# A first attention whose score tiles are no longer computed twice on TensorE

## The reference

```python
# first attention: 16 heads of 16 columns
q, k, v = split((x @ w_in.T + b_in).reshape(b, l, 16, -1), 3, axis=-1)
att = softmax(einsum('blhd,bmhd->blmh', q, k) * 0.25, axis=2)
opt = einsum('blmh,blhd->blhd', att, v)          # m is summed over att alone
x = layernorm(x + opt @ w_out.T + b_out)
# second attention: 4 of 16 heads of 64 columns, chosen for each batch
idx = sort(top_k(softmax(mean(x @ Wr + br, axis=1)), 4))
Qs, Ks, Vs = the chosen heads of x @ Wq + bq, x @ Wk + bk, x @ Wv + bv
O = softmax(Qs @ Ks.T / 8) @ Vs
x = layernorm(x + O @ Wo + bo)
```

## Time and profile before

| | |
|---|---|
| median of 3 runs | 3679.16 us (3677.96 to 3679.68) |
| the profiled execution's own time | 3678.28 us |
| its span, first to last instruction | 3676.2 us |
| TensorE (PE) busy | 3442.9 us (94%) |
| VectorE (DVE) busy | 3328.6 us (91%) |
| ScalarE (ACT) busy | 2863.5 us (78%) |
| mean granted clock of TensorE | 0.983 of full speed |

### The profile page before, as it was taken

The page is one execution under the profiler, slowest core; times in us unless marked ns, Lnnn a source line. Parts: engine busy times, 40 slices in busy tenths (PEclk is TensorE's granted clock), DMA queues, the critical chain, the costliest instruction groups (busy, mean ns, idle before and its releaser), DMA issues. The chain is left out here.

```text
span 3676.2 us, 45342 instructions
## 1 busy us (share of the span) xinstructions
PE 3442.9 (94%) x14524; PEld 1301.0 (35%) x14524; DVE 3328.6 (91%) x5273; ACT 2863.5 (78%) x3137; POOL 1872.8 (51%) x1299
## 2 busy tenths in 40 slices
PE   8999998899999999899999999899999999899998
PEld 3444443332232234343332324343332324343333
DVE  7999999999999998889999998879999998567776
ACT  5999999878888887778888887778888887333333
POOL 4344343414454547455454547445454546658775
PEclk9999999899999999899999999999999999999999
DMA  5222221300000002101010001101000100100000
GB/s 168 92 86 90 86 86 61 87 21 18 18 29 15 23 18 63 54 18 29 18 29 14 26 18 58 59 18 29 18 26 13 29 18 26 43 1 12 12 12 12
DMA packets 117214, 142.83 MB, mean 39 GB/s; under 512 B 33394, under 2 KB 100466, under 8 KB 116978
## 3 DMA queue, kind: packets, MB, share of 16 engines
q1 hardware_dynamic: 116978, 139.95, 12.4%
HBM read 89.55 MB, written 50.33 MB: 38 GB/s over the span
## 5 line engine op out<-in xcount | busy, mean ns | idle before, releaser
L1163 ACT ACTIVATE scores<-scores,nmax 128x2048 f32<-128x2048 f32 x1024 | 2042.4, 1996 | 297.4 <-DVE scores L1391 286.1
L1018 PE MATMUL ps<-stack 96*128 96x512 bf16 x4852 | 1314.0, 388 | 116.2 <-DVE scores L1391 86.2
L1391 DVE TENSOR_SCALAR_CACHE_REDUCE scores<-ps,lows 128x1024 f32<-128x1024 f32 x1024 | 1274.8, 1277 | 45.1 <-PE ps L1018 42.5
L920 POOL TENSOR_TENSOR facc<-facc,probs 128x1024 f32<-128x1024 f32 x443 | 1048.0, 2366 | 487.0 <-ACT probs L1302 416.6
L1391 DVE TENSOR_SCALAR_CACHE_REDUCE scores<-ps 128x1024 f32<-128x1024 f32 x1024 | 1214.6, 1217 | 52.2 <-PE ps L1018 46.9
L1018 PEld LDWEIGHTS ps<-stack 96*128 96x128 bf16 x4852 | 374.5, 99 | 1174.6 <-DVE scores L1391 687.8
L1448 DVE TENSOR_REDUCE smax<-ps 128x2 f32<-128x1024 f32 x512 | 620.3, 1219 | 131.4 <-PE ps L1083 129.9
L1083 PE MATMUL ps<-fk,fq 64*128 64x512 f32 x2048 | 562.5, 631 | 48.5 <-DVE smax L1448 30.9
L1098 PE MATMUL ps<-fq,fk 64*128 64x512 f32 x2048 | 550.2, 615 | 10.0 <-DVE smax L1448 4.1
L1118 PE MATMUL ps<-probs,vals 128*64 128x512 f32 x2048 | 527.4, 612 | 0.2
L1302 ACT ACTIVATE probs<-ps 128x1024 f32<-128x1024 f32 x384 | 383.2, 1012 | 66.9 <-PE ps L1101 66.4
(11 more groups left out here) (136 smaller groups left out, 2335.5 us busy)
## 6 DMA issues: line engine op xcount, KB each, us to landing
stack<-qk_levels SPq DMA_DIRECT2D x768, 64.0 KB, 2.2
qk_levels<-fk SPq DMA_DIRECT2D x64, 384.0 KB, 2.4
probs<-in_L_attn_x SPq DMA_DIRECT2D x16, 512.0 KB, 3.9
v_rows<-vals SPq DMA_DIRECT2D x16, 512.0 KB, 2.6
vrows<-v_rows SPq DMA_DIRECT2D x16, 512.0 KB, 3.4
res<-in_L_attn_x SPq DMA_DIRECT2D x16, 512.0 KB, 3.9
x_rows<-y SPq DMA_DIRECT2D x16, 512.0 KB, 2.9
res<-x_rows SPq DMA_DIRECT2D x16, 512.0 KB, 3.9
```

The costliest lines, as they stand in the source:

```text
L920: pool.tensor_tensor(total, total, probs[:, slot, :], ALU.add).then_inc(facc_ready, 1)
L1018: last = pe.matmul(bank(banks[i]), stack[0:SK, hd % 2, 0, t * P:(t + 1) * P], stack[0:SK, hd % 2, 1, col:col + CH], start=True, stop=True)
L1163: act.activation(row, row, ACT.Exp, bias=nmax[:, k % LOWS:k % LOWS + 1], scale=-1.0, accum_out=esum[:, b % 2, t, hd:hd + 1]).then_inc(exp_ ...
L1391: dve.tensor_scalar(scores[:, k % ROW_SLOTS, half * TILE:(half + 1) * TILE].rearrange("p (a n) -> p a n", a=2), two_banks(banks), 1.0, fir ...
```

## The change

The rule, the set and the second matmuls go. `plan()` no longer adds 0.43 us to any tile, so its simulated TensorE is free earlier, and the orders that it writes differ from the first doubled tile on. The line numbers of what follows fall by up to 5 (L1018 becomes L1013, L991 L986, L985 L980, L976 L971, L1055 L1050).

```diff
-NEAR = 12
...
-    again = set()
...
-                twice = n[1] == "A" and queued and not any(m[1] in mode for m in order["PE"][-NEAR:])
-                if twice:
-                    again.add(n)
-                switch = 0.43 * twice + 0.1 * (mode.get(n[1], 0) != now_mode)
+                switch = 0.1 * (mode.get(n[1], 0) != now_mode)
...
-    return order, held, freed, again, now
+    return order, held, freed, now
...
-        order, held, freed, again, planned = plan()
+        order, held, freed, planned = plan()
...
-                    for i in (0, 1, 0, 1) if n in again else (0, 1):
+                    for i in (0, 1):
```

## The result

The changed kernel takes 3702.6 us in the median of 4 runs (3700.39 to 3705.82), the kernel before 3678.86 (3677.96 to 3679.68): a ratio of 1.0065, 95% interval [1.0053, 1.0077]. It is slower by 24 us; the forecast was 18 us more than before, at 3697.

A forecast was written before the change was run, and what follows sets the result against it. The prediction took VectorE's reading of tiles to bound batch 0's first attention. Chunks +12 and seams +6 made +18 us on 3678.3, about 3697 beside the median; its own range was 3685 to 3723 us (0.63).

The forecast's parts named there:

- The bound: Batch 0's first attention: it ends when VectorE has read its tiles, one per 1.175 us; freed TensorE time is worth nothing.
- The clock falls in plain runs, and that alone is free: Batch 0's first attention: clock at 0.50 in longer plain runs; a tile then takes 0.94 us, under VectorE's 1.175.
- The price of a chunk: Batch 0's first attention, twelve chunks: low-clock projections cost 1.5 us in 9, +12 net; ends -1.4 and +36.
- the event: Profile before, near 305 us: one q projection at low clock made VectorE wait 1.08 and 0.36 us, 1.44 together.
- I put this at nothing: Batch 0's first attention: packed projections come closer together on ScalarE, 95% busy; expected cost nothing.
- either way: Batch 0's first attention: VectorE starts a tile every 1.175 us with or without the second matmuls.
- The seams, +6: Seams of batches 0, 1 and 2: FK projections start at low clock, +2 us each; ends -5.4 and +9.
- A: Rival, chance 0.23: nothing late, as the clock stays up or ready tiles cover low projections; about 3677 us.
- B: Rival, chance 0.10: faster, since doubled tiles were in the way of the seams; about 3667 us.
- C: Rival, chance 0.04: TensorE becomes the bound at low clock throughout batch 0's first attention; +122 us, 3800.

The follow-up runs named there:

- warm-start kernel: Changed kernel with second matmuls only for the last six tiles before a chunk's transposes and those between transposes and q projection (137 tiles): 3693.06 us, 1.0046.

## Why the prediction was right, and where it was not

- **The bound.** Right. Batch 0's first attention ends when VectorE has read its tiles, and the TensorE time that was freed (146 us by the prediction's estimate at full clock) bought nothing there.
- **The clock falls in plain runs, and that alone is free.** Right, and shown: 68.1 us at 0.50 with VectorE busy throughout, and in the warm-start kernel low clock almost without waits.
- **The price of a chunk: 1.5 us for 9 of 12, +12 in all.** The stage lost 16.4 us, inside the ends given (-1.4 to +36), but the term was made up wrongly. Late tiles rose by 6.5 us at most (3.0 to 9.5), not 12. I had let the clock be down at the q projection nine times; it was down four times, and at the other eight chunks the clock had come back behind the transposes. In those four chunks lie 7.3 of the 8.2 us of waits, 1.8 us each instead of 1.5. Part of each price is ScalarE's, which I had not seen in my own rows: the second wait of the event, 0.36 us before 306.89, also ends 0.12 us behind ScalarE's reading, with the tile ready.
- **"I put this at nothing" (ScalarE, with the packed projections).** This is the step that failed. It has two parts. ScalarE's list is fixed, and at the low clock it stands idle for the transposes (4.4 us against 1.1 before) and the projections (7.4 against 2.0); with it the waits for its rows rise by some 3 us, and by some 2 more that the profile calls late tiles. It is the low clock that makes ScalarE late and not, as I had it, the packing. And the planner's new order has VectorE take 38 second halves of batch 0 right behind their first halves: +6.6 us. The prediction let VectorE start a tile every 1.175 us "either way"; I read only TensorE's order, and VectorE's would have shown the pairs. The two misses, 6 us too much and 10 too little, cancel in part: that the total came within 6 us of the measured one is in part luck.
- **The seams, +6.** Too much for the place: +2.5 us from the 481st tile to the second attention after batch 2's seam. The mechanism was right where it was named: in batch 0's seam the FK projections started low (5.29 us for 8 records, 3.67 before) and VectorE waited 4.56 us for 2.93. But single tiles gave back as much before it, so that seam ends 1.0 us better than it began. Some 5 us were lost later, in the last batch, where the forecast had nothing; their cause stays open.
- **The rivals.** A (nothing late) and B (a gain in the seams) did not come; that doubled tiles can stand in the way of a seam shows in the kernel with more of them, but the seams' own 70 were a gain of 5.5 us. C did not come either: with transposes and projections the clock came back each time.

The rows at 744.48 and 750.24 us of the changed kernel, for the FK projections:

```profile
744.48 5.29 PE L986 MATMUL ps<-x1T,wqk_sel 128*128 128x512 f32 x8 [2.41 <-DVE scores L1386]
```
```profile
750.24 1.22 DVE L1386 TENSOR_SCALAR_CACHE_REDUCE scores<-ps 128x1024 f32<-128x1024 f32 x1 [4.56 <-PE ps L1013]
```

## What to carry to other kernels

Work that computes nothing can still pay: look at what the clock does where an engine off the path gets thinner, and ask which heavier work meets the low level next. In this kernel filling was worth it just ahead of such work; in the seams, where the filled engine is itself awaited, more of it cost more than the clock returned. Look also for a third engine between the two: here ScalarE waited for the slow work and passed the delay on. And when a planner's cost changes, read the new order of every engine, the bound one first.

## What the runs showed of the hardware

TensorE's clock fell to 0.50 in a run of matmuls with no gap longer than 0.81 us before it, and stayed there for 68.1 us, with gaps of 0.17 us. On VectorE, the same 128 x 1024 tile took 1281 ns with a minimum from an SBUF column as its scalar and 1219 ns without, an estimated 61 us over the kernel; and an instruction that waits for the one just before it on its own engine started 0.2 us later.
